# Attention with a span mask and a ternary feed-forward layer: value projection in float32r parts, prologue and last pair in another order

## The chip, the cores and the metric

The kernel runs on one core of a Trainium2 chip. TensorE (PE) multiplies matrices, with weight loads (PEld in the rows) and matmuls as separate instructions; VectorE (DVE) and ScalarE (ACT) read its results in PSUM; GpSimd (POOL) works on SBUF alone; SyncE (SP) issues DMAs. The metric is device microseconds of one execution, as the median of several runs; lower is better.

## The reference

Four sequences of 1024 rows with 128 features are normalised; attention with 16 heads of 64 and a quantised ternary linear layer are both computed from the normalised rows and added to the input.

```python
xn = layernorm(x)                                   # x: 4 x 1024 x 128
q, k, v = split_heads(xn @ Wq), split_heads(xn @ Wk), split_heads(xn @ Wv)   # 16 heads of 64
w = softmax(q @ k^T / 64 + causal)
mask = clip((arange(1024) + span_val * 1024) / 33, 0, 1)     # one span_val per head
w = w * mask;  w = w / (sum(w) + 1e-8)
attn = merge_heads(w @ v) @ Wo
x_int = clip(round(xn / scale), -127, 127)
ffn = nan_to_num(x_int * scale) @ (ternary - 1)^T + bias
out = x + attn + ffn
```

## The kernel before

The work is 32 head pairs: 4 batches of 8 pairs, a pair being two heads of 64 that lie one above the other in the 128 partitions. Each engine walks through a hand-written list of units, once per pair i; a `+` behind a unit's name means that it belongs to pair i+1, a `-` to pair i-1. The lists are PE_PLAN, ACT_PLAN, DVE_PLAN and POOL_PLAN, and for the prologue PE_FIRST, DVE_FIRST and ACT_FIRST. Semaphores tie the engines together, so an engine always waits at the head of its own list. There is no scheduler.

A pair goes as follows. Q and K (`projection`, L817 to L819) multiply the weights by the transposed rows. Both sides are kept as two float32r parts, high and low, and three products (high by high, high by low, low by high) of 512 columns each stand for a full-precision one. ACT takes the high part out of PSUM (Qhi, Khi, L477), DVE the rest (Qlo, Klo, L645). M0 to M11 (`max_unit`, L840) compute scores from the high parts alone, only so that DVE can find each row's maximum (R0 to R11, L668 and L672); T (L847) transposes the maxima, DVE copies them (Tc, L686) and a DMA puts them in a row of `mrow`. S0 to S11 (`scores_of`, L867) compute the transposed scores of one block of 128 keys against up to 512 queries, for both heads, each in its half of the rows of the array: three products of the parts, and a fourth with `kext` and `mrow`, which subtracts the maximum and adds the logarithm of the key's weight. Tiles 0 to 3 are the first half of the queries, 4 to 11 the second; tiles 0 to 3 and 8 to 11 lie on the diagonal and have 512, 384, 256 and 128 columns. E0 to E11 (L488) take the exponential on ACT. POOL zeroes the triangle (L0 to L11, L407) and adds the probabilities of a half in `psumd` (A0 to A11, L426 to L432). G3, G7 and G11 (`value_products`, L884) multiply by the values. D0 and D1 (L893) sum `psumd` over the keys with a matmul by ones. Ln and Exp on ACT (ln, ex) and three DVE steps (t, u, o) turn that into the normalised output of the half, Y0 and Y1 (L910) project it, and DVE adds it to the row (Ya). In a batch's last pair the feed-forward products of that half (L906) go ahead of Y.

V (`values`, L827) computes the values of a pair: for each of 8 blocks of 128 rows one fp32 matmul, 128 rows as the stationary tile, 128 columns of Wv as the moving one. DVE multiplies the result by the key table (Vs, L654). q is one of seven steps by which DVE quantises a batch (L590 to L602), one per pair; Z is a step of the next batches' layer norm; X0 and X1 turn the next batch's rows.

Scores, projections, V and maxima share three slots of PSUM (`ring`, two banks each) in the order in which PE comes to them: a unit waits until the unit three places ahead of it has been read (`slot_left`). T, D, Y, X and the feed-forward products share one bank (`beside`), and the value products have one (`pv`).

Prologue: DVE zeroes `kext` and `mrow` (L716, L717), POOL fills rows of them with -1 and 1 (L346, L348), splits the first 128 columns of Wq and Wk (L354, L359), computes the key weights (L369 to L385) and splits the rest of the weights; DVE makes the key masks (L628 to L638) and the quantisation scale (L571 to L580). On PE the prologue is Q, K, M0 to M11 and V of pair 0; everything of pair 1 follows in the plan of pair 0.

## Time and profile before

| what | value |
|---|---|
| median of 3 runs | 1027.01 us (1025.49 to 1027.22) |
| the profiled execution | 1027.36 us |
| its span | 1025.6 us |
| PE busy, share of the span | 989.4 us, 96% |
| DVE busy | 781.4 us, 76% |
| POOL busy | 735.0 us, 72% |
| ACT busy | 452.7 us, 44% |
| PE's share of the chain that ended last | 92% |

The span is what the profiler's records cover; the execution's time is 1.8 us more. Busy shares are means over stages. The times of matmuls in the rows overlap, since matmuls are pipelined; what one costs in a stream is the distance of two starts, not the length of its record. Times in the rows are counted from the span's start.

### The profile page before, as it was taken

Reading aid. Unit: us, or ns where it says so; the run is one execution under the profiler, and the core shown is the slowest. Engines: PE = TensorE matmul, PEld = TensorE weight load, DVE = VectorE, ACT = ScalarE, POOL = GpSimd, SP = SyncE. Lnnn points to the kernel's source line nnn. Section 1 sums busy time; section 2 is a strip of 40 time slices with the busy share of each in tenths; the row PEclk is TensorE's granted clock in tenths of the full one; section 3 lists DMA queues with packets and bytes.
Section 4 is the critical chain, followed back from the end, with each engine's and each line's share of the span. In section 5 each row is a group of like instructions: output and inputs, shape, how many; then the busy total and the mean of one; then the engine's idle time right before and its main releaser. Section 6 shows DMA issues by size and latency. Waiting matters only on the chain.

```text
span 1025.6 us, 19261 instructions
## 1 busy us (share of the span) xinstructions
PE 989.4 (96%) x7169; PEld 636.0 (62%) x7169; DVE 781.4 (76%) x1753; ACT 452.7 (44%) x600; POOL 735.0 (72%) x646
## 2 busy tenths in 40 slices
PE   3699999999999999999999999999999999999996
PEld 2466666666666666666666666666666666666654
DVE  8778888888788888877768777777877777777752
ACT  2144544444544444544444544444454444454441
POOL 8686766777776677776867676768776667767685
PEclk9599999999999999999999999999999999999998
DMA  6000000000000000000000000000000000000000
...
DMA packets 12124, 8.44 MB, mean 8 GB/s; under 512 B 1280, under 2 KB 11520, under 8 KB 12032
## 3 DMA queue, kind: packets, MB, share of 16 engines
...
q14 instruction: 35, 0.29, 0.1%
...
## 4 chain that ended last, share of the span: by engine, by line
PE 92%; DVE 3%; POOL 2%; issue 2%; DMA 1%; ACT 1%; POOLq 0%; SPq 0%; DVEq 0%
PE ring L867 28%; PE pv L884 23%; PE ring L840 10%; PE beside L910 7%; PE ring L827 6%; PE beside L893 6%; PE ring L817 3%; PE ring L818 3%; PE ring L819 3%; POOL psumd L432 1%; DVE rowmax L672 1%; PE beside L906 1%; PE beside L847 1%; DMA x_sb<-in_L_attn_query 0%; POOL psumd L428 0%
## 5 line engine op out<-in xcount | busy, mean ns | idle before, releaser
L488 ACT ACTIVATE prob<-ring 128x1024 f32<-128x1024 f32 (+3 forms) x384 | 297.5, 812 | 350.5 <-PE ring L867 342.3
L432 POOL TENSOR_TENSOR psumd<-psumd,prob 128x1024 f32<-128x1024 f32 (+3 forms) x256 | 429.5, 1678 | 29.2 <-POOL psumd L432 1.3
L668 DVE CUSTOM_DVE_ANT_0 ring<-ring,causal 128x128 f32<-128x128 f32 (+3 forms) x512 | 240.4, 517 | 114.4 <-PE ring L840 114.0
L867 PE MATMUL ring<-q,k 64*128 64x512 f32 (+3 forms) x2304 | 284.7, 353 | 3.6 <-DVE rowmax L672 2.0
L884 PE MATMUL pv<-prob,v 128*64 128x512 f32 (+3 forms) x1536 | 267.0, 490 | 0.0
L407 POOL TENSOR_SCALAR_AFFINE_SELECT prob<-prob 128x256 f32<-128x256 f32 x256 | 104.1, 407 | 198.6 <-ACT prob L488 196.0
L867 PEld LDWEIGHTS ring<-q,k 64*128 64x128 f32 x2304 | 189.8, 186 | 48.8 <-ACT prob L488 10.6
L884 PEld LDWEIGHTS pv<-prob,v 128*64 128x64 f32 x1536 | 104.7, 137 | 154.1 <-issue 141.1
L672 DVE TENSOR_REDUCE rowmax<-ring 128x2 f32<-128x1024 f32 x128 | 153.3, 1219 | 17.4 <-PE ring L840 14.1
L428 POOL TENSOR_TENSOR psumd<-prob 128x768 f32<-128x768 f32 x64 | 134.2, 2097 | 42.4 <-ACT prob L488 37.4
L840 PE MATMUL ring<-k,q 64*128 64x512 f32 (+3 forms) x768 | 143.7, 411 | 6.8 <-ACT k L477 2.4
L867 PE MATMUL ring<-mrow,kext 64*128 64x512 f32 (+3 forms) x768 | 133.4, 343 | 0.0
L840 PEld LDWEIGHTS ring<-k,q 64*128 64x128 f32 x768 | 65.5, 186 | 68.8 <-ACT prob L488 26.7
L477 ACT ACTIVATE q<-ring 128x1024 fp32r<-128x1024 f32 x32 | 32.9, 1028 | 167.5 <-PE ring L819 167.5
L867 PEld LDWEIGHTS ring<-mrow,kext 64*128 64x128 f32 x768 | 73.1, 186 | 8.3
L645 DVE TENSOR_TENSOR q<-ring,q 128x1024 fp32r<-128x1024 f32 x32 | 39.1, 1222 | 47.1 <-ACT q L477 47.0
L910 PE MATMUL beside<-wo,o 128*128 128x128 f32 x512 | 74.1, 288 | 0.2 <-DVE o L703 0.2
L668 DVE DVE_READ_ACCUMULATOR2_ANT rowmax<- 128x1 f32 x512 | 72.7, 142 | 0.1
L910 PEld LDWEIGHTS beside<-wo,o 128*128 128x128 f32 x512 | 62.8, 193 | 14.0 <-issue 10.4
L893 PE MATMUL beside<-psumd,ones 128*64 128x512 f32 x256 | 69.0, 617 | 1.9 <-POOL psumd L432 1.9
L827 PE MATMUL ring<-wv,xf 128*128 128x128 f32 x512 | 67.4, 286 | 0.0
L827 PEld LDWEIGHTS ring<-wv,xf 128*128 128x128 f32 x512 | 61.2, 196 | 8.1 <-issue 7.3
...
## 6 DMA issues: line engine op xcount, KB each, us to landing
...
kext<-lnw SPq DMA_DIRECT2D x64, 8.0 KB
mrow<-maxrow SPq DMA_DIRECT2D x64, 4.0 KB
...
```

The source lines that it names most:

```text
L407: g.affine_select(out=d, in_=d, compare_op=ALU.is_ge, fill=0.0, base=0, pattern=[[0, 2], [1, P]], channel_multiplier=-1).then_inc(sel_done, 1)
L428: g.tensor_tensor(acc[:, :, lo:HALF], before[:, :, lo:HALF], pr[:, :, lo:HALF], ALU.add).then_inc(acc_done, 2)
L432: g.tensor_tensor(acc[:, :, lo:HALF], acc[:, :, lo:HALF], pr[:, :, lo:HALF], ALU.add).then_inc(acc_done, 1)
L488: a.activation(prob[n % NPROB][:, :, lo:HALF], ring[:, slot(f"S{t}", i), :, lo:HALF], ACT.Exp, scale=1.0 / DH).then_inc(exp_done, 1)
L668: last = v.tensor_tensor_reduce(out=ring[:, s, h, 0:n], in0=ring[:, s, h, 0:n], in1=causal[:, HALF - n:HALF], scale=1.0, scalar=MASKED, op ...
L672: last = v.tensor_reduce(dst[:, :, 0], ring[:, s, :, 0:n], axis=AX, op=ALU.max)
L827: last = t_.matmul(ring[:, s, kb // HB, (kb % HB) * P:(kb % HB + 1) * P], xf[i // NPB % 2][:, kb * P:(kb + 1) * P], wv[:, (i % NPB) * P:(i ...
L840: last = t_.matmul(ring[:, s, h, 0:n], q1[p][rows, j * P:(j + 1) * P], k1[p][rows, k0:k0 + n], start=True, stop=True)
L867: last = t_.matmul(ring[:, s, h, lo:HALF], k[p][rows, keys], q[p][rows, cols], start=(at == 0), stop=(at == len(parts) - 1))
L884: last = t_.matmul(pv[h * DH:(h + 1) * DH, lo:HALF], v_sb[p][:, kb, h, :], prob[(i * NT + t) % NPROB][:, h, lo:HALF], start=(kb == 0), sto ...
L893: last = t_.matmul(beside[h * DH:(h + 1) * DH, :], ones[:, :], psumd[c][:, h, :], start=True, stop=True)
L910: last = t_.matmul(beside[:, k * P:(k + 1) * P], o_sb[c][:, k * P:(k + 1) * P], wo[:, i % NPB, :], start=not with_ffn, stop=(not with_ffn ...
```

## The change

**Value projection.** Wv is split in two float32r parts, wv1 (ACT) and wv2 (POOL), as Wq and Wk are. For each block of 128 rows V is now three float32r matmuls of 128 columns: rows' high part by wv1, by wv2, and rows' low part by wv1. The fp32 copy of the rows, xf, serves the quantisation alone, in one buffer.

**Prologue.** ACT makes the high parts of the weights. POOL makes the key masks, in 16 operations of eight columns, and fills two rows of -1 and 1 that eight DMAs copy into `kext` and `mrow`; Wv is loaded after the rest of Wq and Wk. ACT does the scaling and splitting of the logarithms. DVE's quantisation scale comes ahead of the normalisation. Q starts on the rows' high part (x1) and waits for the low part only before its third product. PE runs eight idle fp32 matmuls (identity by `causal`, into `pv`) before the first transposes. Q and K of pair 1 and S0 to S2 of pair 0 are in the prologue's list; V of pair 0 stands behind them.

**q** moves on DVE from ahead of R6 to behind o0.

**Last pair.** PE_LAST and POOL_LAST replace the plans. POOL adds no more than tile 7 of the second half; D1 takes tiles 8 to 11 directly from the probabilities (`direct`) and lies in the ring. The feed-forward products of the second half (F1) are a unit of their own ahead of G7, and G11 stands behind D1.

```diff
-DVE_PLAN = ("Tc Z Qlo+ Klo+ R0+ R1+ X0 X1 W R2+ R3+ t1- Vs+ u1- R4+ o1- R5+ Ya1- q R6+ R7+ t0 u0 R8+ o0 R9+ "
-            "R10+ Ya0 R11+ Rc+")
+DVE_PLAN = ("Tc Z Qlo+ Klo+ R0+ R1+ X0 X1 W R2+ R3+ t1- Vs+ u1- R4+ o1- R5+ Ya1- R6+ R7+ t0 u0 R8+ o0 q "
+            "R9+ R10+ Ya0 R11+ Rc+")
-PE_FIRST = "Q+ K+ M0+ M1+ M2+ M3+ M4+ M5+ M6+ M7+ M8+ M9+ M10+ M11+ V+"
-ACT_FIRST = "Qhi+ Khi+ keys+"
+PE_FIRST = ("Q+ K+ M0+ M1+ M2+ M3+ M4+ M5+ M6+ M7+ M8+ M9+ M10+ M11+ Q++ T+ K++ S0+ S1+ S2+ V+")
+DVE_FIRST = ("keys+ Qlo+ Klo+ R0+ R1+ R2+ R3+ R4+ R5+ R6+ R7+ R8+ R9+ R10+ R11+ Rc+ Tc+ Qlo++ Klo++ Vs+")
+ACT_FIRST = "xf0+ Qhi+ xf1+ Khi+ rest+ keys+ wv+ Qhi++ Khi++ E0+ E1+ E2+"
+PE_LAST = "T G11- S0 S1 S2 D1- S3 S4 S5 Y1- S6 S7 D0 G3 S8 S9 S10 Y0 S11 F1 G7 D1 G11 Y1"
+POOL_LAST = "L0 A0 L1 A1 L2 A2 L3 A3 A4 A5 A6 L8 L9 L10 A7 L11"
...
             def values(i):
...
-                pe.wait_ge(wv_landed, 16)
+                pe.wait_ge(wv_lo_done, 1)
+                cols = slice((i % NPB) * P, (i % NPB + 1) * P)
+                xa, xb = x1[i // NPB % 2], x2[i // NPB % 2]
                 for kb in range(KB):
-                    last = t_.matmul(ring[:, s, kb // HB, (kb % HB) * P:(kb % HB + 1) * P],
-                                     xf[i // NPB % 2][:, kb * P:(kb + 1) * P], wv[:, (i % NPB) * P:(i % NPB + 1) * P],
-                                     start=True, stop=True)
+                    out = ring[:, s, kb // HB, (kb % HB) * P:(kb % HB + 1) * P]
+                    rows = slice(kb * P, (kb + 1) * P)
+                    t_.matmul(out, xa[:, rows], wv1[:, cols], start=(kb % HB == 0), stop=False)
+                    t_.matmul(out, xa[:, rows], wv2[:, cols], start=False, stop=False)
+                    last = t_.matmul(out, xb[:, rows], wv1[:, cols], start=False, stop=(kb % HB == HB - 1))
...
                     if name == "Q":
-                        pe.wait_ge(x2_done, 2 * (i // NPB) + c + 1)
+                        pe.wait_ge(x1_done, 2 * (i // NPB) + c + 1)
                     rows = slice(c * HALF, (c + 1) * HALF)
                     xa, xb = x1[i // NPB % 2], x2[i // NPB % 2]
                     t_.matmul(ring[:, s, c, :], w1[n][:, cols], xa[:, rows], start=True, stop=False)
-                    t_.matmul(ring[:, s, c, :], w1[n][:, cols], xb[:, rows], start=False, stop=False)
-                    last = t_.matmul(ring[:, s, c, :], w2[n][:, cols], xa[:, rows], start=False, stop=True)
+                    t_.matmul(ring[:, s, c, :], w2[n][:, cols], xa[:, rows], start=False, stop=False)
+                    if name == "Q":
+                        pe.wait_ge(x2_done, 2 * (i // NPB) + c + 1)
+                    last = t_.matmul(ring[:, s, c, :], w1[n][:, cols], xb[:, rows], start=False, stop=True)
...
             def denominators(i, c):
...
+                direct = range(NT - HB, NT) if c == 1 and i == LAST else ()
+                pe.wait_ge(acc_done, tiles_upto(i, HB - 1 if c == 0 else NT - HB - 1 if direct else NT - 1))
...
+                for t in direct:
+                    lo = first_col(t)
+                    pe.wait_ge(sel_done, i * NDIAG + DIAG_UPTO[t])
+                    for h in range(2):
+                        last = t_.matmul(out[h * DH:(h + 1) * DH, lo:HALF], ones[:, :],
+                                         prob[(i * NT + t) % NPROB][:, h, lo:HALF], start=False, stop=(t == NT - 1))
...
+            for n in range(NIDLE):
+                t_.matmul(pv[:, 0:HALF], ident[:, :], causal[:, :], start=True, stop=True)
...
+            def weights(dst, src, landed, value, done):
+
+                act.wait_ge(landed, value)
+                a.activation(dst, src, ACT.Copy).then_inc(done, 1)
...
+            g.tensor_scalar(span_b[:, :], span_b[:, :], float(S), None, ALU.mult).then_inc(key_step, 1)
+            for n in range(2):
+                rest_of_weights(n, slice(0, P), n + 1)
...
+            for h in range(H):
+                g.tensor_scalar(mask[:, h // 2, :, h % 2], key_no[:, :], span_b[:, h:h + 1], 1.0 / (RAMP + 1),
+                                ALU.add, ALU.mult).then_inc(key_step, 1)
...
+            g.tensor_tensor(wv2[:, :], wv_raw, wv1[:, :].bitcast(F32), ALU.subtract).then_inc(wv_lo_done, 1)
```

PE before, in the prologue, from the last maxima unit of pair 0 to the projections of pair 1 (names are output<-inputs; w_0 and w_1 the parts of the query and key weights, L840 the maxima units, L827 V, L847 T, L817 to L819 the projections):

```order
L840 MATMUL ring<-k_0,q_0 128x512 x2
L827 MATMUL ring<-wv,xf 128x128 x8
L847 MATMUL beside<-ident,rowmax 128x128
L817 MATMUL ring<-x_0,w_0 128x512
L818 MATMUL ring<-x_0,w_0 128x512
```

PE after, from the end of Q of pair 1 to V of pair 0 (L863 to L867 the projections, L899 T, L919 the scores, L879 to L881 V; what is left out repeats these forms):

```order
L867 MATMUL ring<-x_0,w_0 128x512
L899 MATMUL beside<-ident,rowmax 128x128
L863 MATMUL ring<-x_0,w_1 128x512
...
L919 MATMUL ring<-q_0,k_0 128x256 x6
L919 MATMUL ring<-mrow,kext 128x256 x2
L879 MATMUL ring<-wv,x_0 128x128
L880 MATMUL ring<-wv,x_0 128x128
L881 MATMUL ring<-wv,x_0 128x128
```

Q of pair 1 now stands ahead of T of pair 0 and K behind it; V of pair 0 has gone behind the scores S0 to S2, and where it was 8 matmuls it is eight times the last three rows.

DVE before, around q in pair 0 (L672 are maxima of R4 to R7, L691 and L696 are t0 and u0):

```order
L672 TENSOR_REDUCE rowmax<-ring 128x2 x2
L590 TENSOR_SCALAR fq<-xf,sc 128x1024
L672 TENSOR_REDUCE rowmax<-ring 128x2 x2
L691 TENSOR_TENSOR beside<-beside,r 128x512
L696 SCALAR_TENSOR_TENSOR rden<-beside,r 128x512
```

DVE after, the same step (L646 is q, L750 is o0, L714 are R8 and R9):

```order
L714 ISA ring,rowmax_1<-ring,causal 128x128
L714 ISA rowmax_1 128x1
L750 SCALAR_TENSOR_TENSOR o<-pv,rden 128x512
L646 TENSOR_SCALAR fq<-xf,sc 128x1024
L714 ISA ring,rowmax_1<-ring,causal 128x256
```

q has moved past R6, R7, t0, u0, R8 and o0.

PE before, at the program's end (L884 the value products, L893 D1, L906 the feed-forward products, L910 Y1):

```order
L884 MATMUL pv<-prob,v 64x512 x10
L884 MATMUL pv<-prob,v 64x384 x2
L884 MATMUL pv<-prob,v 64x256 x2
L884 MATMUL pv<-prob,v 64x128 x2
L893 MATMUL beside<-psumd,ones 64x512 x2
L906 MATMUL beside<-ternT,fq 128x128 x4
L910 MATMUL beside<-wo,o 128x128 x4
```

PE after, the same units (L963 F1, L936 the value products, L948 and L954 D1, L975 Y1):

```order
L963 MATMUL beside<-ternT,fq 128x128 x4
L936 MATMUL pv<-prob,v 64x512 x8
L948 MATMUL ring<-psumd,ones 64x512 x2
L954 MATMUL ring<-prob,ones 64x512 x2
L954 MATMUL ring<-prob,ones 64x384 x2
L954 MATMUL ring<-prob,ones 64x256 x2
L954 MATMUL ring<-prob,ones 64x128 x2
L936 MATMUL pv<-prob,v 64x512 x2
L936 MATMUL pv<-prob,v 64x384 x2
L936 MATMUL pv<-prob,v 64x256 x2
L936 MATMUL pv<-prob,v 64x128 x2
L975 MATMUL beside<-wo,o 128x128 x4
```

F1 has moved ahead of G7, D1 has eight more matmuls, and G11 stands between D1 and Y1.

## Rows read from the trace of the kernel before

**Rows 1.** The page: busy time by engine, and the chain's shares.

```profile
PE 989.4 (96%) x7169; PEld 636.0 (62%) x7169; DVE 781.4 (76%) x1753; ACT 452.7 (44%) x600; POOL 735.0 (72%) x646
...
PE 92%; DVE 3%; POOL 2%; issue 2%; DMA 1%; ACT 1%; POOLq 0%; SPq 0%; DVEq 0%
```

**Rows 2.** Windows (stretch, length, busy by engine, clock) of one pair; two transposes, timeline.

```profile
866.20:896.20 30.00, 30.00 (x223) 19.20 (x221) 22.61 (x50) 13.79 (x18) 21.42 (x20) 1.00 0.01 2
...
806.09 0.33 PE L847 MATMUL beside<-ident,rowmax 128*128 128x128 f32 x1
...
986.21 0.33 PE L847 MATMUL beside<-ident,rowmax 128*128 128x128 f32 x1
```

**Rows 3.** Timeline (start, length, instruction, count): V and S3; two projection matmuls.

```profile
875.87 1.86 PEld L827 LDWEIGHTS ring<-wv,xf 128*128 128x128 f32 x16 [0.24 <-issue]
...
877.85 0.41 PEld L867 LDWEIGHTS ring<-q,k 64*128 64x128 f32 x6
...
318.03 0.39 PE L818 MATMUL ring<-x,w 128*128 128x512 f32 x1
318.26 0.40 PE L819 MATMUL ring<-x,w 128*128 128x512 f32 x1
```

**Rows 4.** Groups by line, weight loads from 60 to 1017 us (busy us, mean ns).

```profile
L867 PEld LDWEIGHTS ring<-q,k 64*128 64x128 f32 x2262 | 185.3, 185 | 47.0 <-ACT prob L488 10.2 <-DVE rowmax L668 7.1 <-DVE rowmax L672 2.8
...
L827 PEld LDWEIGHTS ring<-wv,xf 128*128 128x128 f32 x480 | 55.8, 191 | 7.3 <-issue 7.3
L817 PEld LDWEIGHTS ring<-x,w 128*128 128x128 f32 x120 | 24.1, 200 | 3.8
L818 PEld LDWEIGHTS ring<-x,w 128*128 128x128 f32 x120 | 22.6, 189 | 3.9
```

**Rows 5.** Timeline of the prologue, and its clock from 44 to 46 us (windows).

```profile
15.97 3.63 POOL L377 TENSOR_SCALAR fq<-fq 16x1024 f32<-16x1024 f32 x1
...
17.07 2.61 DVE L630 TENSOR_SCALAR mask<-key_no,span_b 128x8 f32<-128x8 f32 x16
...
22.90 0.29 DVE L668 CUSTOM_DVE_ANT_0 ring<-ring,causal 128x128 f32<-128x128 f32 x1
...
34.70 0.29 DVE L679 TENSOR_TENSOR rowmax<-rowmax,rowmax 128x8 f32<-128x8 f32 x1
...
35.97 0.42 PE L847 MATMUL beside<-ident,rowmax 128*128 128x128 f32 x1
...
38.65 0.27 DVE L686 CAST maxrow<-beside 16x128 fp32r<-16x128 f32 x1
...
40.77 0.77 PE L817 MATMUL ring<-x,w 128*128 128x512 f32 x1 [4.39 <-issue]
...
44.00:46.00 2.00, 1.42 (x6) 0.81 (x4) 1.16 (x1) 1.28 (x2) 0.00 (x0) 0.91 0.00 0
...
47.80 1.65 PE L867 MATMUL ring<-q,k 64*128 64x512 f32 x6 [0.67 <-DVE k L645]
```

**Rows 6.** Timeline of the last pair.

```profile
986.47 2.37 PE L884 MATMUL pv<-prob,v 128*64 128x512 f32 x16
...
1007.75 6.58 POOL L432 TENSOR_TENSOR psumd<-psumd,prob 128x1024 f32<-128x1024 f32 x4
...
1014.48 1.08 PE L893 MATMUL beside<-psumd,ones 128*64 128x512 f32 x4 [1.86 <-POOL psumd L432]
...
1020.24 1.92 PE L910 MATMUL beside<-wo,o 128*128 128x128 f32 x8
```

**Rows 7.** Timeline: q and S8 in pair 24; R9 and S11 in pair 27.

```profile
792.74 2.71 DVE L590 TENSOR_SCALAR fq<-xf,sc 128x1024 f32<-128x1024 f32 x1
...
797.78 0.96 PE L867 MATMUL ring<-q,k 64*128 64x512 f32 x6 [0.67 <-DVE rowmax L672]
...
890.80 0.43 DVE L668 CUSTOM_DVE_ANT_0 ring<-ring,causal 128x256 f32<-128x256 f32 x1 [1.26 <-PE ring L840]
...
892.14 0.45 PE L867 MATMUL ring<-q,k 64*128 64x128 f32 x6
```

More of the change, by code:

```diff
@@ L72, in happens, with walk @@
     return True
-def walk(plan, first=""):
+def walk(plan, first="", last=None):
+    seen = set()
     for i in range(-1, N_PAIRS + 1):
-        for word in (first if i < 0 else plan).split():
+        for word in (first if i < 0 else plan if last is None or i < LAST else last).split():
             name = word.rstrip("+-")
-            pair = i + (1 if word[-1] == "+" else -1 if word[-1] == "-" else 0)
-            if 0 <= pair < N_PAIRS and happens(name, pair):
+            pair = i + word.count("+") - word.count("-")
+            if 0 <= pair < N_PAIRS and happens(name, pair) and (name, pair) not in seen:
+                seen.add((name, pair))
                 yield name, pair
-IN_RING = [("X", -2)] + [u for u in walk(PE_PLAN, PE_FIRST) if u[0][0] in "QKSMV"]
-IN_BESIDE = [u for u in walk(PE_PLAN, PE_FIRST) if u[0][0] in "TDYXW"]
+PE_ORDER = list(walk(PE_PLAN, PE_FIRST, PE_LAST))
+IN_RING = [("X", -2)] + [u for u in PE_ORDER if u[0][0] in "QKSMV" or u == ("D1", LAST)]
+IN_BESIDE = [u for u in PE_ORDER if u[0][0] in "TDYXWF" and u not in (("D1", LAST), ("Y1", LAST))]
 PLACE = {u: n for n, u in enumerate(IN_RING)}
@@ L257, in slot, with den_bank @@
             return PLACE[name, i] % NSLOT
+        def den_bank(i, c):
+            return ring[:, slot("D1", i), 0, :] if ("D1", i) in PLACE and c == 1 else beside[:, :]
         def tiles_upto(i, t):
@@ L493, in logarithms @@
                 act.wait_ge(den_ready, halves_upto(i, c))
[L494 removed]
+                a.activation(lnden[:, :], den_bank(i, c), ACT.Ln).then_inc(lnden_done, 1)
             def inverses(i, c):
@@ L499, in inverses, with key_logarithms @@
                 a.activation(r0[:, :], lnden[:, :], ACT.Exp, scale=-1.0).then_inc(r0_done, 1)
+            def key_logarithms():
+                act.wait_ge(wgt_done, 1)
+                a.activation(fq[0:H, :], fq[0:H, :], ACT.Ln, bias=eps16[:, 0:1]).then_inc(lnw_done, 1)
+                act.wait_ge(lnw_done, 1)
+                a.activation(fq[0:H, :], fq[0:H, :], ACT.Copy, scale=float(DH)).then_inc(lnw_done, 1)
+                act.wait_ge(lnw_done, 2)
+                a.activation(lnw[:, 0, :], fq[0:H, :], ACT.Copy).then_inc(lnw_split, 1)
+            for n in range(2):
+                weights(w1[n][:, 0:P], w_raw[n][:, 0:P], w_first_landed, 32, w_hi_done)
             rstd_start(1, slice(0, KB))
             for c in range(2):
-                turned(0, c, ring[:, slot("X", -2), c, :])
+                turned_high(0, c, ring[:, slot("X", -2), c, :])
             for name, i in walk(ACT_PLAN, ACT_FIRST):
@@ L514, in _ @@
                 elif name[0] == "X":
-                    turned(batch_of_turn(i), int(name[1:]), beside[:, :])
+                    turned_high(batch_of_turn(i), int(name[1:]), beside[:, :])
+                    turned_whole(batch_of_turn(i), int(name[1:]), beside[:, :])
+                elif name[:2] == "xf":
+                    turned_whole(0, int(name[2:]), ring[:, slot("X", -2), int(name[2:]), :])
+                elif name == "rest":
+                    for n in range(2):
+                        weights(w1[n][:, P:H * DH], w_raw[n][:, P:H * DH], w_rest_landed, 32, w_hi_done)
                 elif name == "keys":
-                    act.wait_ge(wgt_done, 1)
-                    a.activation(fq[0:H, :], fq[0:H, :], ACT.Ln).then_inc(lnw_done, 1)
+                    key_logarithms()
+                elif name == "wv":
+                    weights(wv1[:, :], wv_raw, wv_landed, 16, wv_hi_done)
                 elif STEP_OF[i] == "rstd1":
@@ L901, in output_projection @@
                     pe.wait_ge(wo_landed, 16)
-                if with_ffn:
-                    pe.wait_ge(ternT_done, 1)
-                    pe.wait_ge(fq_step, (i // NPB + 1) * FQ_STEPS)
-                    for k in range(HB):
-                        t_.matmul(beside[:, k * P:(k + 1) * P], fq[:, c * HALF + k * P:c * HALF + (k + 1) * P],
-                                  ternT[:, :], start=(k == 0), stop=False)
+                if with_ffn and (f"F{c}", i) not in PLACE_BESIDE:
+                    feed_forward(i, c)
                 pe.wait_ge(o_done, halves_upto(i, c))
```

160 lines of the change are left out of this document (85 added, 75 removed).

## The prediction

> **What bounds the kernel now.** I read the page's head and chain first. TensorE (PE) is busy for 96% of the span, and 92% of the chain of work that ended last is PE [rows 1]. A busy PE can still be a waiting PE, so I looked at one head pair late in the run, where nothing but attention is done: from one transpose of the maxima (L847) to the next it takes 30.00 us, PE is busy for all of it, VectorE (DVE) for 22.6, GpSimd (POOL) for 21.4 and ScalarE (ACT) for 13.8. The last six such distances make (986.21-806.09)/6 = 30.02 us each, though DVE does quantisation steps of different length beside them, so nothing but PE sets them [rows 2]. A microsecond put on PE in a pair is a microsecond of span, about 31 times. Outside this steady part there are two stretches where PE is not the bound: a prologue, in which the first scores start only at 47.80 us [rows 5], and the last pair, in which POOL's sums of the probabilities end last [rows 6]. The change touches all three, so I price each.
>
> **Value projection in the steady part.** Before, a V unit is 8 fp32 matmuls, shown as 16 pairs of a weight load and a matmul record. The 16 loads last from 875.87 for 1.86 us and one load's own record is 0.19, so a load follows a load every (1.86-0.19)/15 = 0.111 us; from V's start to the start of the next unit it is 877.85-875.87 = 1.98 us [rows 3]. After, it is 3 x 8 = 24 float32r matmuls with a 128x128 stationary tile and 128 moving columns, one record each. The question is the distance of two of those. The trace has float32r matmuls with 128 moving columns in score tile S3, right behind V: six loads, in three pairs of row halves, take 0.41 us, so one pair of halves, side by side in the array, takes (0.41-0.19)/2 = 0.11 us. [...] That a full-array float32r load is no shorter is seen in the projections: its record is 189 ns long, that of V's fp32 loads 191, that of the half-array loads 185. A shared stationary tile does not help: L817 and L818 both use the first part of the weights, and each has its 120 loads [rows 4]. So the unit goes from 16 to 24 steps of 0.111 us: 8 x 0.111 = 0.89 us more, 2.87 in place of 1.98. Nothing covers it, since DVE's reading of V and the units behind it shift as a whole. For 31 of the 32 V units (pair 0's is in the prologue): **+27.6 us**; with steps of 0.105 and 0.115 as ends, 26 to 28.5.
> [...]
>
> **Quantisation step q moved on DVE.** It now stands behind o0 instead of ahead of R6. In pair 24 the longest step, 2.71 us, held R6 and R7 back, and PE waited 0.67 us for them before S8; against a usual pair S8 came 0.83 late [rows 7]. Behind o0, DVE is free for 1.26 us before R9 at 890.80. A 2.7 us step sticks out of that by 1.45; R9 takes about 0.87 and S11, which takes M9's slot and started at 892.14, waits until about 893.2: 1.1 lost, so +0.3 for each of four such steps. Steps of 1 us fit into the gap; the two of 1.6 us per batch stick out by 0.3, for which I take 0.05 to 0.2 each, eight times. Sum **+1.5 us** (0 to 3). The turning of the later batches gains or loses nothing: xf is one buffer now, but freed by a step four pairs earlier.
>
> **Prologue.** What set 47.80 before [rows 5]: POOL split the first weights behind eight memsets and Q0 waited for x2; DVE's masks (2.61 us from 17.07) held Qlo back, the maxima began at 22.90 and ran DVE without a gap to their last at 34.70 (11.8 us); V0 at the low clock ran until T0 came at 35.97, DVE copied T0's result only at 38.65 behind table work, and Q1 and K1 waited for POOL's second weight split until 40.77.
> After, step by step. The scale work (1.3 us on DVE, half of it beside ACT's two short steps) stands ahead of the normalisation: the turned rows come 0.8 later, at 12.8. Eight idle fp32 matmuls of 512 columns run on PE from about 2.3 us. None of that kind is in the trace; as two records of 0.43 us each (twice what 512 float32r columns take) they are 6.9 us, twice that at the low clock. In the prologue the clock rose 3.6 us after PE took up work at 40.77 (the mean level of 44 to 46 is 0.91); at that price they end near 11, ahead of the rows, at worst 3.3 us behind them. Q0 then starts on x1 alone, near 14.1, and Q0 and K0 take 0.23 a matmul instead of 0.43: K ready near 18.0, its high part by 19.3. POOL however has the key masks now: one operation of 1.1 us, 16 small ones (0.2 to 0.5 each by POOL's smallest rows; 0.25 since eight columns are near the low end), the clamp of 3.63 us (15.97) and two short ones. Keys are ready near 17.9, and DVE's reciprocal, first in its list, holds Qlo to 19.3 and R0 to 21.7. That is 1.2 earlier than 22.90; at 0.5 an operation it is 3 later. The maxima take the same 11.8 us. Q1 runs beside their end, T0 follows at once, its copy is not behind table work, and with the DMA (2.6 us from copy to landing) S0 starts near **37 us** in place of 47.8: 10.7 earlier.
> That is not all gain. V0 (2.9 us) and M0, M1 of pair 1 (0.4), done ahead of 47.80 before, come after it. And there is a new wait: behind V0, PE has only four short maxima units (1.3 us) until V1, and these need slots that DVE frees: Vs0 1.2, statistics 1.6, R0 and R1 1.2 together. From V0's end DVE needs about 4.2 us to free V1's slot, so PE stands for 2.9 us. 10.7-2.9-0.4-2.9 = **-4.5 us** (0 to -8).
>
> **Last pair.** POOL no longer adds tiles 8 to 11 of half 1 (most of the 6.58 us from 1007.75) [rows 6]; PE takes them with ones against the probabilities, at the price of G11, the same four shapes (2.37 us with its tail, 2.1 without). F1 goes ahead of G7 (1.0 us), and S6 now stands behind Y1, which waits for o1, so PE idles 0.9 more there. From G7's end near 1012.3, D1 with its psumd part (0.9) then ends at 1015.3, where it ended at 1015.56: PE has taken POOL's place as the bound. From there ACT and DVE need the same 2.8 us; G11 runs beside them. Behind o only Y1 is left, at the high clock (1.1 us), where Y1 at the low clock took 1.92 and began at 1020.24, 1.2 after o, because F1 was ahead of it. The end comes **2 us** earlier (0 to 4).
>
> **Sum.** Against the profiled execution, 1027.36 us with its span of 1025.6, 0.35 above the median: 1027.4 + 27.6 + 1.5 - 4.5 - 2.0 = **1050 us**. The ends of the terms, not all at once, give 1040 to 1056.
>
> **Rivals.** (a) The stream paces V, not the load: if the load of a full-array float32r tile hides, a step is 0.06 us, V takes 24 x 0.06 + 0.2 = 1.7, 0.25 less than before, and the time is 1027.4 - 7.8 + 1.5 - 4.5 - 2.0 = 1015: faster. It decides below 0.08 us a step, where V's extra no longer outweighs the 5 us of the three other terms. For it: no full-array float32r matmul of 128 columns is in the trace. Against it: load records of one length in all three kinds, and the score tiles' 0.11 [rows 3, 4]. 7%. (b) The load hides in part, a step between the two, (0.06+0.11)/2 = 0.085: V takes 24 x 0.085 + 0.2 = 2.24, +8 us in all, 1030. [...] 5%. (c) The load price holds, but waits within the pair absorb half of it: 1027.4 + 13.8 - 5 = 1036. Against: PE busy throughout the 30.00 us [rows 2]. 4%. (d) POOL's masks or the idle matmuls come out dear, and the prologue loses 3 us or more: above 1056. 6%. (e) The change does not do what it says, each added matmul keeps fp32's two records: 48 steps, 32 x 0.111 x 31 = 110 us more. 1%. The forecast, 1040 to 1056, has 77%.
>
> **Chances.** A measurement of this kernel tells about 0.2% (2 us) from no change. Faster: (a) and a little of (b), 8%. Same: 3%. Slower: 89%. The range 1038 to 1056 holds about 8 in 10.
>
> **What would show it.** In the changed trace V's 24 loads should last 2.7 to 2.8 us in all, and late in the run two L847 should be 30.9 us apart; 29.75 shows (a), 30.3 (b), 30.45 (c). S0 should start near 37 us, with a PE gap of some 3 us before V1; S11 should wait for R9 in pairs 0, 8, 16 and 24; behind the last D1 only ACT and DVE should stand ahead of Y1. I am wrong if a float32r load in the full array is shorter than its record says.

## The result, and the profile after

The changed kernel takes 1051.49 us (median of 4 runs, 1050.99 to 1052.5), the kernel before in the same job 1026.28. The ratio is 1.0246, its 95% interval 1.0229 to 1.0264: slower by 2.5%. The profiled execution took 1050.99 us with a span of 1049.2, 23.6 more than the 1025.6 of before.

The page after, its busy times and the chain's shares, beside [rows 1]:

```profile
span 1049.2 us, 19835 instructions
PE 1026.1 (98%) x7457; PEld 669.0 (64%) x7457; DVE 770.9 (73%) x1734; ACT 457.7 (44%) x607; POOL 709.0 (68%) x650
...
PE 94%; DVE 2%; POOL 1%; issue 1%; DMA 1%; ACT 0%; SPq 0%; DVEq 0%; ACTq 0%
```

PE is busy for 36.7 us more, the span is only 23.6 longer: elsewhere PE stands less. The other engines have a little less to do. The windows of two pairs late in the run (stretch, length, busy time of PE, PEld, DVE, ACT and POOL, clock), from L899 (T) to L899:

```profile
887.92:918.81 30.89, 30.89 (x231) 20.09 (x229) 22.54 (x50) 13.80 (x18) 21.18 (x20) 1.00 0.01 2
918.81:949.66 30.85, 30.85 (x231) 20.10 (x229) 23.21 (x50) 13.80 (x18) 21.53 (x20) 1.00 0.01 2
```

These answer to the 30.00 us of [rows 2]: 0.87 us more in a pair, DVE and POOL as before. Inside that pair stands V, here its first, second and last record and the unit behind it (timeline of PE), and one group of its weight loads over the whole run:

```profile
897.60 0.33 PE L879 MATMUL ring<-wv,x 128*128 128x128 f32 x1
897.76 0.28 PE L880 MATMUL ring<-wv,x 128*128 128x128 f32 x1
...
900.22 0.27 PE L881 MATMUL ring<-wv,x 128*128 128x128 f32 x1
900.42 0.55 PE L919 MATMUL ring<-q,k 64*128 64x128 f32 x6
...
L881 PEld LDWEIGHTS ring<-wv,x 128*128 128x128 f32 x240 | 46.1, 192 | 0.0
```

The 24 matmuls start 897.60 to 900.22, (900.22-897.76)/22 = 0.112 us apart (0.111 by the starts of their loads, which is the figure used below), and the next unit starts 2.82 us behind V's start, where it was 1.98 [rows 3]. The load record is 192 ns long, the 191 of fp32 [rows 4].

The transposes L899 cut the span into three parts. All 23.6 us are in them:

| part | before | after | difference |
|---|---|---|---|
| start to T of pair 1 | 72.87 | 75.35 | +2.5 |
| T of pair 1 to T of pair 31 | 913.34 | 936.15 | +22.8 |
| T of pair 31 to the end | 39.39 | 37.66 | -1.7 |

At 0.87 us a pair the middle would be 26.1 longer; 3.3 are missing. 2.8 of them lie in pairs 8, 16 and 24, where the longest q step stands: these take 32.04, 31.77 and 31.75 us, and took 32.07, 31.81 and 31.83 before. DVE in pair 24 after, beside [rows 7], and POOL's next instruction:

```profile
818.86 0.69 DVE L750 SCALAR_TENSOR_TENSOR o<-pv,rden 128x512 f32<-128x512 f32 x1
819.46 0.74 DVE L646 TENSOR_SCALAR fq<-xf,sc 128x1024 f32<-128x1024 f32 x1
820.81 0.43 DVE L714 CUSTOM_DVE_ANT_0 ring<-ring,causal 128x256 f32<-128x256 f32 x1 [0.60 <-PE ring L892]
...
820.25 0.41 POOL L432 TENSOR_SCALAR_AFFINE_SELECT prob<-prob 128x256 f32<-128x256 f32 x1 [1.85 <-ACT prob L525]
```

The step that took 2.71 us takes 0.74 here, POOL is idle for 1.85 us around it, and DVE still waits 0.60 before R9: nothing is held back.

The prologue (timelines of POOL, DVE and PE; POOL's masks, DVE's first steps and first maximum, S0, the two waits before V of pair 1, and that V's first two records):

```profile
9.16 6.00 POOL L401 TENSOR_SCALAR mask<-key_no,span_b 128x8 f32<-128x8 f32 x16
15.25 3.63 POOL L404 TENSOR_SCALAR fq<-fq 16x1024 f32<-16x1024 f32 x1
...
20.14 0.95 DVE L683 RECIPROCAL wrec<-wrec 128x128 f32<-128x128 f32 x1 [4.96 <-POOL wrec L408]
21.13 1.16 DVE L684 TENSOR_TENSOR vtab<-mask,wrec 128x128 f32<-128x128 f32 x1
...
24.60 0.29 DVE L714 CUSTOM_DVE_ANT_0 ring<-ring,causal 128x128 f32<-128x128 f32 x1
...
40.27 0.96 PE L919 MATMUL ring<-q,k 64*128 64x512 f32 x6 [0.71 <-DMA mrow<-maxrow]
...
46.81 0.44 PE L892 MATMUL ring<-k,q 64*128 64x384 f32 x2 [0.89 <-DVE v L700]
49.19 0.64 PE L892 MATMUL ring<-k,q 64*128 64x512 f32 x2 [1.94 <-DVE rowmax L714]
49.95 0.47 PE L879 MATMUL ring<-wv,x 128*128 128x128 f32 x1
50.23 0.41 PE L880 MATMUL ring<-wv,x 128*128 128x128 f32 x1
```

and the windows over the same place (clock behind the five busy times):

```profile
44.00:50.00 6.00, 3.05 (x23) 2.07 (x22) 4.25 (x18) 0.00 (x0) 3.84 (x5) 0.95 0.00 0
50.00:58.00 8.00, 8.00 (x42) 7.48 (x44) 3.45 (x9) 0.38 (x1) 1.04 (x2) 0.50 0.00 0
```

S0 starts at 40.27, 7.5 us earlier than at 47.80 [rows 5], but all of that and 2.5 more is gone when T of pair 1 comes. DVE waits 4.96 us for POOL's key table before it starts on Qlo. Behind PE's waits of 0.89 and 1.94 us the granted clock is 0.50 from 49.4 to 59.6 us, and V of pair 1 goes at 0.213 us a step.

The end, beside [rows 6] (timeline of PE): D1's two parts, G11 and Y1.

```profile
1037.84 1.03 PE L948 MATMUL ring<-psumd,ones 128*64 128x512 f32 x4
1038.69 2.32 PE L954 MATMUL ring<-prob,ones 128*64 128x512 f32 x16
1040.85 2.32 PE L936 MATMUL pv<-prob,v 128*64 128x512 f32 x16
1044.56 1.16 PE L975 MATMUL beside<-wo,o 128*128 128x128 f32 x8 [1.39 <-DVE o L750]
```

No wait for POOL stands ahead of D1 any more, and Y1 takes 1.16 us where it took 1.92.

### The profile page after: what moved, and what is told of

Same layout as the page of the kernel before. It is cut to its first block, busy times and chain, and to the rows that moved or that the text cites. A ratio compares the mean times of both kernels' runs of the same rounds, so it can differ in the third digit from the quotient of the medians.

```text
span 1049.2 us, 19835 instructions
## 1 busy us (share of the span) xinstructions
PE 1026.1 (98%) x7457; PEld 669.0 (64%) x7457; DVE 770.9 (73%) x1734; ACT 457.7 (44%) x607; POOL 709.0 (68%) x650
## 4 chain that ended last, share of the span: by engine, by line
PE 94%; DVE 2%; POOL 1%; issue 1%; DMA 1%; ACT 0%; SPq 0%; DVEq 0%; ACTq 0%
PE ring L919 28%; PE pv L936 24%; PE ring L892 10%; PE beside L975 7%; PE beside L948 6%; PE ring L879 3%; PE ring L881 3%; PE ring L880 3%; PE ring L863 3%; PE ring L867 3%; PE ring L864 3%; PE beside L963 1%; PE beside L899 1%; DVE rowmax L718 0%; POOL mask L401 0%
## 5 line engine op out<-in xcount | busy, mean ns | idle before, releaser
L459 POOL TENSOR_TENSOR psumd<-psumd,prob 128x512 f32<-128x512 f32 (+1 forms) x252 | 410.1, 1627 | 27.7
L714 DVE CUSTOM_DVE_ANT_0 ring<-ring,causal 128x128 f32<-128x128 f32 (+3 forms) x512 | 240.5, 517 | 96.2 <-PE ring L892 95.4
L919 PE MATMUL ring<-q,k 64*128 64x512 f32 (+3 forms) x2304 | 284.0, 353 | 1.6 <-DMA mrow<-maxrow 1.4
L936 PE MATMUL pv<-prob,v 128*64 128x512 f32 (+3 forms) x1536 | 267.2, 490 | 0.0
L432 POOL TENSOR_SCALAR_AFFINE_SELECT prob<-prob 128x256 f32<-128x256 f32 x256 | 107.0, 420 | 231.5 <-ACT prob L525 229.3
L919 PEld LDWEIGHTS ring<-q,k 64*128 64x128 f32 x2304 | 191.0, 186 | 45.2 <-ACT prob L525 12.4
L936 PEld LDWEIGHTS pv<-prob,v 128*64 128x64 f32 x1536 | 104.7, 137 | 153.6 <-issue 139.9
L919 PE MATMUL ring<-mrow,kext 64*128 64x512 f32 (+3 forms) x768 | 133.6, 343 | 0.0
L919 PEld LDWEIGHTS ring<-mrow,kext 64*128 64x128 f32 x768 | 73.6, 186 | 8.1
L975 PE MATMUL beside<-wo,o 128*128 128x128 f32 x512 | 73.4, 286 | 2.5 <-DVE o L750 2.5
L879 PE MATMUL ring<-wv,x 128*128 128x128 f32 x256 | 73.1, 286 | 0.1
L714 DVE DVE_READ_ACCUMULATOR2_ANT rowmax<- 128x1 f32 x512 | 72.6, 142 | 0.1
L975 PEld LDWEIGHTS beside<-wo,o 128*128 128x128 f32 x512 | 62.0, 191 | 16.5 <-issue 9.8
L738 DVE TENSOR_TENSOR beside<-beside,r 128x512 f32<-128x512 f32 x63 | 45.1, 715 | 36.2 <-ACT r L536 36.2
L881 PE MATMUL ring<-wv,x 128*128 128x128 f32 x256 | 71.5, 279 | 0.0
L880 PE MATMUL ring<-wv,x 128*128 128x128 f32 x256 | 71.5, 279 | 0.0
```

The lines of the kernel that those rows point to most:

```text
L432: g.affine_select(out=d, in_=d, compare_op=ALU.is_ge, fill=0.0, base=0, pattern=[[0, 2], [1, P]], channel_multiplier=-1).then_inc(sel_done, 1)
L459: g.tensor_tensor(acc[:, :, lo:HALF], acc[:, :, lo:HALF], pr[:, :, lo:HALF], ALU.add).then_inc(acc_done, 1)
L714: last = v.tensor_tensor_reduce(out=ring[:, s, h, 0:n], in0=ring[:, s, h, 0:n], in1=causal[:, HALF - n:HALF], scale=1.0, scalar=MASKED, op ...
L879: t_.matmul(out, xa[:, rows], wv1[:, cols], start=(kb % HB == 0), stop=False)
L880: t_.matmul(out, xa[:, rows], wv2[:, cols], start=False, stop=False)
L919: last = t_.matmul(ring[:, s, h, lo:HALF], k[p][rows, keys], q[p][rows, cols], start=(at == 0), stop=(at == len(parts) - 1))
```

## The experiments

The theory after the result had four parts. L: V is paced by the loads of its stationary tile, 0.111 us for 128 columns. Q: q gains, because this DVE step is slow only while POOL works (2.71 us before, 0.74 here). K: in the prologue the key table on POOL holds DVE back. C: the waits in front of V of pair 1 (0.89 and 1.94 us) bring the clock down (0.50), and that costs more than the waits. Each kernel is the changed kernel with the edit shown; `...` stands for lines left out. The kernel before took 1027.1 to 1027.6 us in the jobs of the experiments and 1026.3 in that of the changed kernel, so a difference between the medians of two jobs is uncertain by about 1 us; what is finer is read from the traces.

**e1, V back in fp32.** What feeds V goes back with it: xf has two buffers again, ACT copies Wv whole, and POOL does not split it. All else is as changed.

```diff
...
-                    t_.matmul(out, xa[:, rows], wv1[:, cols], start=(kb % HB == 0), stop=False)
-                    t_.matmul(out, xa[:, rows], wv2[:, cols], start=False, stop=False)
-                    last = t_.matmul(out, xb[:, rows], wv1[:, cols], start=False, stop=(kb % HB == HB - 1))
+                    last = t_.matmul(ring[:, s, kb // HB, (kb % HB) * P:(kb % HB + 1) * P],
+                                     xf[i // NPB % 2][:, kb * P:(kb + 1) * P], wv[:, cols],
+                                     start=True, stop=True)
...
```

> The changed kernel with V alone put back to 8 fp32 matmuls (xf in two buffers again, Wv copied whole by ACT, no split on POOL). Theory L (a load of 128 columns paces V at 0.111 us a step): the V unit falls from 24 to 16 steps, pairs of 30.87 us become 30.0, and V of pair 1, which ran at the low clock, gets 1.7 us shorter: 1051 - 31 x 0.87 - 1.7 = about 1022 us, below the kernel before. Rival: most of the 25 us comes from elsewhere in the new order (waits around V, the last pair, the prologue), then the time stays above 1035.

Measured 1021.83 us, ratio 0.9951 (0.9937 to 0.9964). The pairs are back at 30.0. The value projection alone accounts for 29.7 of the change between the medians, 28.2 between the profiled executions; the rest of it gains 5.3 against before: T of pair 1 comes at 72.61 (before 72.87), pairs 1 to 30 take 910.70 (913.34, q), the end 37.65 (39.39). This splits the 22.8 us by which the middle grew: against e1 the float32r V makes it 25.5 longer (0.85 a pair), and the rest, q above all, makes it 2.6 shorter than before.

**e2, 256 moving columns in place of 128, still 24 matmuls.** The values that come out are no longer V; only the time counts.

```diff
-                cols = slice((i % NPB) * P, (i % NPB + 1) * P)
+                cols = slice(min(i % NPB, NPB - 2) * P, (min(i % NPB, NPB - 2) + 2) * P)
...
-                    out = ring[:, s, kb // HB, (kb % HB) * P:(kb % HB + 1) * P]
+                    at = kb % HB // 2 * 2
+                    out = ring[:, s, kb // HB, at * P:(at + 2) * P]
...
```

> The changed kernel with the 24 matmuls of V moving 256 columns instead of 128 (work added; the values that come out are not the reference's). Theory L: the stream of 256 columns, 0.107 us, still nearly hides behind the load, a step goes from 0.111 to about 0.115 us, +0.1 us a pair, 1053 to 1055 us. Rival F (a float32r matmul costs its stream of 0.053 us and a fixed 0.058 beside it, in series): a step is 0.165 us, +1.3 us a pair, about 1091 us.

1056.95 us (one run), a step of 0.119 us, pairs of 31.1. Twice the columns cost 0.008 us a step. At 128 columns it is not the moving side that sets the pace. The expectation's 0.107 and 0.053 us for a stream of 256 and 128 columns are estimates: in the kernel before, the 512-column matmuls of Q of pair 1 start (43.47-41.77)/4 = 0.425 us apart at a granted clock of 0.50, and a half and a quarter of that, halved again for a clock of 1.00, are 0.106 and 0.053.

**e3, 64 columns of stationary tile in place of 128, moving side as it was.** Half of the values are left out.

```diff
-                    out = ring[:, s, kb // HB, (kb % HB) * P:(kb % HB + 1) * P]
+                    out = ring[0:DH, s, kb // HB, (kb % HB) * P:(kb % HB + 1) * P]
-                    rows = slice(kb * P, (kb + 1) * P)
+                    rows = slice(kb * P, kb * P + DH)
```

> The changed kernel with 64 of a block's 128 rows as V's stationary tile, so that a load has 64 columns; still 24 matmuls of 128 moving columns (half of the values are left out). Theory L: the load is halved to about 0.055 us and a step becomes 0.06 to 0.07 us, 1.0 to 1.2 us less a pair, 1015 to 1021 us. Rival F' (each matmul has a cost of 0.11 us whatever it loads): V stays at 24 steps of 0.111 us, 1051 us.

1018.48 us (one run). Its weight loads by group, and its waits of PE from 100 to 960 us (total, times, longest):

```profile
L881 PEld LDWEIGHTS ring<-wv,x 128*64 128x64 f32 x240 | 32.4, 135 | 0.0
...
PE ring L892 <- DVE v L700: 5.8, 28, 0.2
```

Half the load, 0.060 us a step where the full tile has 0.111, and a load record of 135 ns where that has 192: with e2 that settles L. 0.060 is a little more than half of 0.111. But the pair became 29.95 us and not the 30.87 - 24 x 0.052 = 29.6 that half the load should give. PE waited 0.2 us in 28 pairs for DVE's reading of V, which no trace had shown so far; the last 0.1 stands before Y1. I come back to this at e9.

**e4, q back where it was.**

```diff
-DVE_PLAN = ("... Ya1- R6+ R7+ t0 u0 R8+ o0 q R9+ R10+ Ya0 R11+ Rc+")
+DVE_PLAN = ("... Ya1- q R6+ R7+ t0 u0 R8+ o0 R9+ R10+ Ya0 R11+ Rc+")
```

> The changed kernel with the quantisation step q back ahead of R6 on DVE. [...] Rival from the prediction (the duration is the step's own, only its place changed): the steps keep their 0.7 to 1.4 us and the time is within 1 us of 1051.

By Q the longest step should be back at 2.7 us, and the time at about 1054. Measured: 1054.04 us, ratio 1.0263 (1.0249 to 1.0277), 2.55 more than changed. Pairs 8, 16 and 24 take 32.89, 32.59 and 32.60 us for 32.04, 31.77 and 31.75. DVE, then POOL, at q of pair 24 in this kernel (timelines):

```profile
816.12 2.67 DVE L646 TENSOR_SCALAR fq<-xf,sc 128x1024 f32<-128x1024 f32 x1
...
815.86 5.15 POOL L459 TENSOR_TENSOR psumd<-psumd,prob 128x1024 f32<-128x1024 f32 x2
...
821.11 0.96 PE L919 MATMUL ring<-q,k 64*128 64x512 f32 x6 [0.61 <-DVE rowmax L718]
```

The same instruction, 2.67 us beside two POOL sums that began 0.26 us earlier, 0.74 us beside an idle POOL; over four batches 2.42 on average against 0.75. From T of pair 1 to T of pair 31 the trace is 2.5 us longer. 815.86 + 5.15/2 is 818.4, so q ends little behind the first of the two sums. Q holds: the place is what counts. By what the sums hold the step up, no run shows.

**e5, the key table behind the maxima on DVE.**

```diff
-DVE_FIRST = ("keys+ Qlo+ Klo+ R0+ ... R11+ Rc+ Tc+ Qlo++ Klo++ Vs+")
+DVE_FIRST = ("Qlo+ Klo+ R0+ ... R11+ Rc+ Tc+ keys+ Qlo++ Klo++ Vs+")
```

> The changed kernel with DVE's two steps on the key table (reciprocal and product, which wait for POOL's masks) moved from the head of its prologue list to behind Tc. Theory K (POOL's masks are what starts the maxima late): R0 starts near 19.5 us instead of 24.6, S0 near 35.2 instead of 40.3, the time falls by 4 to 5.2 us to about 1046.5. Rival: something else of the prologue (POOL's split of the rest of the weights, the DMA of the key weights, the low clock) is late next and takes the gain, then less than 2 us come off.

1046.98 us, ratio 1.0195 (1.0178 to 1.0212), 4.5 less than changed. DVE's first steps there (timeline):

```profile
16.77 1.23 DVE L691 TENSOR_TENSOR q<-ring,q 128x1024 fp32r<-128x1024 f32 x1 [1.66 <-ACT q L514]
18.18 1.23 DVE L691 TENSOR_TENSOR k<-ring,k 128x1024 fp32r<-128x1024 f32 x1 [0.18 <-ACT k L514]
19.32 0.29 DVE L714 CUSTOM_DVE_ANT_0 ring<-ring,causal 128x128 f32<-128x128 f32 x1
```

R0 starts at 19.32 instead of 24.60, T of pair 0 at 31.54 instead of 36.82, T of pair 1 at 70.66 instead of 75.35. K holds.

**e6, three idle matmuls where PE waited.**

```diff
+                if (name, i) in (("M2", 1), ("M3", 1)):
+                    for n in range(1 if name == "M2" else 2):
+                        t_.matmul(pv[:, 0:HALF], ident[:, :], causal[:, :], start=True, stop=True)
```

> The changed kernel with three more idle fp32 matmuls of 512 columns on PE in pair 0, one ahead of M2 and two ahead of M3 of pair 1, where PE waits for DVE for 0.9 and 1.9 us. Theory C (the wait lets PE's clock fall to its low level, and V1 and the scores behind it pay): V1 runs in steps of 0.111 us instead of 0.213, 2.4 us less, and with the units behind it 2.4 to 3.5 us come off, about 1048. Rival: the clock falls anyway or the idle matmuls run past the wait and only add, 1051 to 1053.

1047.41 us, ratio 1.0198 (1.0183 to 1.0214), 4.1 less than changed though PE has more to do. Windows, and V of pair 1 (PE's timeline):

```profile
44.00:50.00 6.00, 6.00 (x33) 3.65 (x32) 3.42 (x14) 0.57 (x2) 4.68 (x5) 1.00 0.00 0
50.00:58.00 8.00, 7.74 (x65) 5.98 (x64) 5.55 (x15) 2.83 (x4) 1.52 (x3) 1.00 0.00 0
...
50.78 0.33 PE L879 MATMUL ring<-wv,x 128*128 128x128 f32 x1 [0.26 <-DVE rowmax L714]
50.95 0.27 PE L880 MATMUL ring<-wv,x 128*128 128x128 f32 x1
```

V of pair 1 starts 0.83 us later than in the changed kernel and ends earlier. From T of pair 0 to T of pair 1 it is 34.25 us instead of 38.54. C holds: the idle time did not go, it was filled, and the clock stayed at 1.00.

**e7, the last pair by the ordinary plans.**

```diff
-PE_ORDER = list(walk(PE_PLAN, PE_FIRST, PE_LAST))
+PE_ORDER = list(walk(PE_PLAN, PE_FIRST))
...
-            for name, i in walk(POOL_PLAN, "", POOL_LAST):
+            for name, i in walk(POOL_PLAN):
...
-                direct = range(NT - HB, NT) if c == 1 and i == LAST else ()
+                direct = range(NT - HB, NT) if False else ()
```

> The changed kernel with the plans of the pairs before also for the last pair (all tiles of half 1 added on POOL, the feed-forward products ahead of Y1, G11 ahead of D1). Theory: from the last transpose of the maxima to the end 39.4 us as before instead of 37.7, +1.7 us, 1052.8. Rival: the new end gives nothing, since PE became the bound in it, 1051.

1053.72 us, ratio 1.0258 (1.0242 to 1.0273), 2.2 more than changed; T of pair 31 to the end is 39.25 us instead of 37.66. PE there waits for POOL again (timeline):

```profile
1041.32 1.08 PE L948 MATMUL beside<-psumd,ones 128*64 128x512 f32 x4 [1.86 <-POOL psumd L459]
1045.21 2.08 PE L963 MATMUL beside<-ternT,fq 128*128 128x128 f32 x8 [2.81 <-DVE rden L743]
1047.08 1.76 PE L975 MATMUL beside<-wo,o 128*128 128x128 f32 x8
```

**e8, without the idle matmuls at the start.** `NIDLE = 0`.

> The changed kernel without the eight idle matmuls at the start. Theory K: Q0 and K0 run at the low clock, K is ready some 2.6 us later, but the maxima wait for the key masks anyway, so R0 moves by less than 0.5 us and the time stays at 1051. Rival: the idle matmuls are worth what they save on PE, 2.5 us, 1053.5.

1052.29 us (one run). Without them Q of pair 0 goes at 0.43 us a matmul, where the changed kernel has 0.23 to 0.35, and M0 of pair 0 starts at 19.56 instead of 18.35. DVE's reciprocal starts at 20.77 instead of 20.14, T of pair 0 comes at 37.46 and T of pair 1 at 76.67. But these three can't be put down to the idle matmuls: e7, with the prologue of the changed kernel, has 20.74, 37.42 and 76.83, and e4 has 20.73, 37.40 and 76.08, where the changed kernel has 20.14, 36.82 and 75.35. The same prologue moves that much from one profiled execution to the next, and its last part with it: from T of pair 0 to T of pair 1 it is 38.5 us here, 38.7 in e4, 39.4 in e7. The 4.3 us that e6 gains there, and e5's 5.3 us at R0, stand clear of this. Since DVE waits for POOL's table anyway, no use of the faster Q is seen. One run can't tell 0.8 us from nothing.

**e9, V for two pairs at a time.** Each V unit computes half of the rows for two pairs, 12 matmuls with 256 moving columns, so every tile loaded serves two pairs. DVE reads it in two steps of 512 columns, into three buffers instead of two. To make room, three small buffers of the denominators are one, so ACT's Ln has to wait for the o ahead of it.

```diff
-                for kb in range(KB):
-                    out = ring[:, s, kb // HB, (kb % HB) * P:(kb % HB + 1) * P]
+                for k in range(HB):
+                    kb = HB * (i % 2) + k
+                    out = ring[:, s, k // 2, (k % 2) * 2 * P:(k % 2 + 1) * 2 * P]
...
```

> The changed kernel with V dealt out over two pairs: one unit computes 4 blocks of rows for two pairs at once, 12 float32r matmuls with 256 moving columns of Wv, where it computed 8 blocks for one pair in 24 with 128; the same products, half as many loads (three value buffers, and the three small buffers of the denominators in one, for space). Theory L: a step is 0.119 us as measured with 256 columns, a unit 12 x 0.119 + 0.2 = 1.63 us in place of 2.87, pairs of 29.6 us, 38 us less over 31 pairs, and V1 at the low clock 2.5 less: 1010 us, below both kernels. Rival: DVE reads V in two instructions now and M4 behind it waits, or the second half of a pair's values comes late, which takes 0.3 us or more of each pair: 1020.

1020.85 us, ratio 0.9939 (0.9924 to 0.9953). The rival was right in the size, pairs are 30.0 us; but its reason, the two reads, is not what does it, since e3 has the wait with a single read. PE (one score unit, M4) and DVE in pair 27 (timelines):

```profile
875.51 0.50 PE L900 MATMUL ring<-k,q 64*128 64x512 f32 x2 [0.25 <-DVE v L705]
...
872.89 0.73 DVE L720 CUSTOM_DVE_ANT_0 ring<-ring,causal 128x512 f32<-128x512 f32 x1
...
873.54 0.73 DVE L744 TENSOR_TENSOR beside<-beside,lnden 128x512 f32<-128x512 f32 x1
874.18 1.27 DVE L705 TENSOR_TENSOR v<-ring,vtab 128x512 f32<-128x512 f32 x2
875.38 0.68 DVE L749 SCALAR_TENSOR_TENSOR lnden<-beside,lnden 128x512 f32<-128x512 f32 x1
876.16 1.23 DVE L724 TENSOR_REDUCE rowmax<-ring 128x2 f32<-128x1024 f32 x1
877.31 0.68 DVE L756 SCALAR_TENSOR_TENSOR o<-pv,lnden 128x512 f32<-128x512 f32 x1
```

V takes 1.62 us from its start to the next unit, 0.36 less than in fp32. But DVE is busy from R3 to o1: it comes to V only at 874.18, PE stands 0.25 us before M4, which takes V's slot, and the last 0.1 goes before Y1, which waits for o1.

**e10, e9 with e5 and e6.**

> V over two pairs, the key table late on DVE and the three idle matmuls in pair 0, all together. If the gains are independent: 1010 less 4.5 less 3.5 = about 1002 us. Rival: with V shorter the wait ahead of V1 is another, the idle matmuls run past it, and only one of the two prologue gains comes: 1006.

1014.16 us, ratio 0.9873 (0.9856 to 0.9889): 6.7 less than e9 for the two prologue edits (4.5 and 4.1 when each was made by itself). The expected 1002 counted on shorter pairs, which e9 had not been measured for yet; they are 30.0.

**e11 and e12: is the floor of 30 us DVE's order or DVE's work?**

```diff
-DVE_PLAN = ("... R2+ R3+ t1- Vs+ u1- R4+ o1- R5+ ...")
+DVE_PLAN = ("... R2+ R3+ Vs+ t1- u1- R4+ o1- R5+ ...")
-PE_PLAN = ("... S5 S6 M5+ Y1- M6+ M7+ ...")
+PE_PLAN = ("... S5 S6 M5+ M6+ Y1- M7+ ...")
```

e12 has the first of the two swaps alone, both stand on e10.

> The kernel of e10_all with two swaps: VectorE reads the value projection ahead of the first step of the denominator of the pair before (Vs ahead of t1), and TensorE's output step of the pair before goes one unit later (Y1 behind M6 instead of behind M5). Question: the value projection of e9 and e10 takes 1.62 us of a pair from its first matmul to the next unit where the fp32 one of e1 took 1.98, and still all three kernels, and e3 with half of the weight loads, keep a pair of 29.95 to 30.0 us. In e9 TensorE waits 0.25 us for VectorE's read of the values before M4 (the read stands behind a step of 0.64 us that had been queued ahead of it), and Y1 starts 0.1 us behind the end of M5. Theory P (a pair is pinned there by VectorE's order alone): with the read first and Y1 later the 0.36 us come through, at least 0.25 of them, pairs of 29.64 to 29.75, 30 pairs bring 7.5 to 11 us, 1003 to 1007 us after 1014.2. Rival Q (VectorE's queue as a whole sets that stretch, it is busy without a pause from the fourth row maximum to o1): the wait moves to the next unit that needs VectorE (M5 behind R4, or Y1 behind o1), pairs stay at 29.95 to 30.0, 1012 to 1015 us.

> The kernel of e10_all with the first of the two swaps alone (VectorE's read of the value projection ahead of the first step of the denominator of the pair before). o1, on which Y1 waits, ends when it ended before, since the same steps stand ahead of it. Theory P (two pins, the read and o1): the wait before M4 goes, the wait before Y1 grows to 0.3 us or so, pairs stay at 29.9 to 30.0, 1011 to 1014.5 us. Rival Q (the read alone is the pin): as e11_read_and_y, 1003 to 1007 us.

e11: 1010.96 us, ratio 0.9839 (0.9824 to 0.9854), the fastest of all. e12: 1017.27, ratio 0.9901 (0.9884 to 0.9917), slower than e10. Waits from 860 to 980 us (total, times, longest), e10, then e11, then e12:

```profile
PE ring L900 <- DVE v L705: 1.0, 4, 0.3
```

```profile
PEld ring L900 <- DVE rowmax L724: 1.6, 4, 0.4
```

```profile
PE beside L985 <- DVE o L756: 0.7, 4, 0.2
```

In both, M4 comes 0.4 us earlier than in e10 (12.76 and 12.77 us behind T instead of 13.16). In e11 0.14 of it is left at M5 (15.20 instead of 15.34), whose loads wait for R4, and the pair is 29.87. In e12 Y1 waits for o1, and the pair is 30.13, longer than in e10's 30.01. DVE in e12, from the end of R3 to u1 (timeline):

```profile
838.17 0.14 DVE L720 DVE_READ_ACCUMULATOR2_ANT rowmax<- 128x1 f32 x1
838.38 1.29 DVE L705 TENSOR_TENSOR v<-ring,vtab 128x512 f32<-128x512 f32 x2
839.58 0.69 DVE L744 TENSOR_TENSOR beside<-beside,lnden 128x512 f32<-128x512 f32 x1
840.31 0.69 DVE L749 SCALAR_TENSOR_TENSOR lnden<-beside,lnden 128x512 f32<-128x512 f32 x1
```

With the read first, DVE comes to it before PE has finished V: it starts 0.21 us behind the last record of R3 (838.17 to 838.38), where t1 in e9 and e10 starts together with that record. And u1 now stands directly behind t1, whose result it takes: 0.73 us from start to start, where t1 and the read behind it were 0.64 apart. o1 so starts 15.08 us behind T and not 14.96, although the same steps stand ahead of it; the expectation had it unchanged. Pairs 1 to 30 take 913.4 us in e12 and 910.4 in e10: 3.0 of the 3.1 us by which e12 is slower. In e11 Y1 stands later and hides this.

So neither theory is right as it stood. P's 29.64 to 29.75 us a pair were not reached, and Q's wait did move to the next unit that needs DVE, but order was still worth 0.13 us a pair and 3.2 in all. What bounds the place is DVE, busy from R3 to o1: that is read from these rows, and no run with less work on DVE there tests it. One read of V instead of two would give little: in e3 the single read takes 1.21 us where e9's two take 1.27, and PE waits the same 0.2 us.

## Why the prediction came out right

The predicted 1050 us stands against 1051.5. Step by step, in the profiled executions:

- **V: 8 more steps of 0.111 us.** Predicted 2.87 us for V and +0.89 in a pair; measured 2.82 and +0.87 (0.85 on average against e1), pairs of 30.87 where 30.9 was named. The step that carried it was to read the pace from score tile S3 and from the length of load records, not from the number of columns. e2 (0.119 us a step with twice the moving columns) and e3 (0.060 with half the tile) show that the load is the cause. Without the V change (e1) the kernel is 5.3 us faster than before. The prediction had 5.0 for the three other terms, but from other places, as the next points show.
- **Rivals (a) and (b)** fell with the step of 0.111 us. The 0.06 us of (a), from which (b)'s 0.085 comes too, was an estimate, a quarter of the 0.23 us between two matmuls of 512 columns [rows 3]; no run shows it for a tile of 128 columns, which takes 0.111, and only the tile of 64 in e3 goes at 0.060. But (a)'s price was wrong too, in two ways. Its sum is off: 24 x 0.06 + 0.2 is 1.64 us, 0.34 less than before and not 0.25, which gives 1012 and pairs of 29.66. And e3, which had that step (V in 1.58 us), took 1018.5 us with pairs of 29.95, since PE then waits for DVE.
- **q: wrong in sign.** Predicted +1.5, measured -2.6 over pairs 1 to 30 (before against e1; e4 gives 2.5 for the place alone). The step that failed is the carrying over of 2.71 us to the new place. [rows 7] gave a length of the step beside a busy POOL, and the new place has an idle one. That S11 would have to wait for R9 did not happen.
- **Prologue: sum wrong.** Predicted, with V of pair 1, -4.5 + 0.9 = -3.6 at T of pair 1; measured +2.5, a miss of 6.1. Two terms: POOL's 16 mask operations took 0.375 us each and not 0.25, and then 3.63, 0.62 and 0.54, so the key table was ready at 20.1 instead of 17.9; DVE's two table steps took 2.1 us instead of 1.4. S0 came at 40.27, not 37: 3.3. The 0.375 us lay within the 0.2 to 0.5 named for an operation. e5 shows that the table set R0. The other 2.8 lie behind S0, where the low clock is enough to account for them. PE's waits were foreseen (2.9 us; 0.89 + 1.94 = 2.83 measured), but only their length was charged. Behind them the clock was 0.50 for 10.2 us and V took 0.213 us a step, where V of pair 0 had 0.111. e6 shows this: same waits filled, 4.1 us back. The 0.43 us for a record of the idle matmuls, and twice that at the low clock, was an estimate; in the changed kernel the loads of these records start 0.85 us apart up to 8.44 and 0.43 behind it, the last at 11.45, and the prediction had the end near 11. In e4 and e7, where nothing of this prologue was changed, the miss at T of pair 1 is 0.7 and 1.5 us larger still.
- **Last pair: right.** Predicted -2, measured -1.7; e7 gives 1.6 in the trace and 2.2 between medians.

In the sum, with V of pair 1 counted to the prologue: V 26.7 predicted and 25.5 measured, q 1.5 and -2.6, prologue -3.6 and +2.5, end -2.0 and -1.7. q lay 2.6 outside the ends given for it (0 to +3), the prologue 1.6 (-8 to 0, and 0.9 for V); their misses of -4.1 and +6.1 cancelled for the most part. V carried the sign and the size of the change; that the total is within 1.0 us in the profiled execution is in part luck.
